# A fused attention and FP4 kernel on eight cores: another order of the quantisation steps, and GpSimd's large operations tied to a step of VectorE

## The chip, the cores and the metric

One Trainium2 chip, eight cores, one launch of the same program on each core. There is no exchange between cores: core i works on batches 2i and 2i+1 of the 16. The time is device microseconds of the slowest core. A comparison of this kernel can tell about 2% from no change.

## The reference

`x` is (16, 2048, 1024) in float32; a core has 4096 rows of it, 32 tiles of 128 rows. Cut to what matters:

```python
xn = layernorm(x)
# s: attention block
qkv = rmsnorm(xn, scale1) @ qkv_w.T
q, k = exp(-0.5*q*q), exp(-0.5*k*k)
out = (q @ (k.T @ v)) / (q @ k.sum() + 1e-6)          # per head, 16 heads of 64
x1  = xn + gamma * (out @ proj_w.T + proj_b)
s   = x1 + gamma * (gelu(rmsnorm(x1, scale2) @ conv1_w.T + conv1_b) @ conv2_w.T + conv2_b)
# g: FP4 feed-forward on the same xn; Q = blockwise FP4 quantise + dequantise, blocks of 16
h = silu(Q(xn) @ Q(w_gate).T) * (Q(xn) @ Q(w_up).T)
g = silu(Q(h) @ Q(w_down).T)
return x + s * g
```

Q takes the largest magnitude of each block of 16, scales by it and rounds to the eight FP4 levels.

## The kernel before

`build()` records every operation with `S.add(engine, fn, waits, ev)` in one global order; each engine then runs its own operations strictly in that order and waits on semaphores for the named events. So an operation that waits holds back everything recorded after it on its engine, and nothing else. The work of a core has three stretches.

**Attention, to about 460 us.** For each tile t: `stats(t)` (two BN_STATS and a BN_AGGR on VectorE, then six small operations on GpSimd that end with `mrs`), `turn(t)` (ScalarE writes the normalised tile `xn1`, SyncE transposes it by DMA), four `kv_group` and, spread over the tiles, `q_group` (eight matmuls each, then ScalarE takes the result out of PSUM), `kv_mm(t)`. SyncE's queue also carries the loads of x (`xa`), the loads of the weights `wst` (`load_w`), the loads `xf` and stores `ob` of the quantisation and the stores of `phi_h`. `cast_w(n)` turns a staged weight into bf16: those of conv1 on ScalarE, those of conv2 and of the projection (16 and 8) on GpSimd as a product with `gm` (L568). `load_w(n)` waits for the cast that held its buffer, on SyncE.

**Attention output and MLP, to about 1030 us.** Eight groups s of four tiles. In the 16 steps oc of `conv1(s, oc)` stand, for the next group's tiles: `prep_xc(t)` (ScalarE normalises x into `xx`, GpSimd adds `gb`, L842), `attn(t)` and `attn_z(t)` (VectorE: den, zz, atz from PSUM), `proj(t)` (x2 on VectorE adds PSUM into `xx`; ScalarE sums the squares; two small operations on GpSimd give rs2) and `proj_xn2(t)` (xn2 on ScalarE, then GpSimd adds `gc2` to `xx`, L945, event x2c). Then `conv2` and `s_out` (VectorE adds PSUM and `xx`).

**FP4 feed-forward, to the end.** Gate, up and down matmuls with `h_task`s in between. Here `late[0]` is true. GpSimd has no work.

**Quantisation.** Each task k is a block of 128 x 1024 (or 768). `stage1`: am (L238), sc (L242), rc (L245), y (L247), all on VectorE; then `coarse` on ScalarE (L256, writes `gam`); `stage2`, VectorE: T (L266, event q_t, reads `gam` and `xf`), nq (L269), out (L272, event q_out, writes `ob`, which SyncE stores). `period(a, b)` interleaves stage1 of task k, letters a, with stage2 of task k-1, letters b, by a string. In the first two stretches `pump(ns)`, called after each group of matmuls, draws as many of these steps as its credit pays for, so the quantisation of the weights and of 17 tiles of x is spread over the matmuls:

```python
            for n, who in enumerate("aabababa" if a.n == 5 else "aababab"):
```

The waits of the ScalarE step are `waits=["q_y%d" % k, opt("q_out%d" % (k - 2))]`.

Of the kernel before, what the change touches and what calls it, by code (L numbers as in the profile page):

```python
# [68 lines left out]
def build():  # L69
    S = Sched()  # L70
# [14 lines left out]
    with ExitStack() as es:  # L85
# [59 lines left out]
        gc2 = gm  # L145
# [63 lines left out]
        late = [False]  # L209
        KX = 28  # L210
# [19 lines left out]
        def stage1(k, W, first, src_ev):  # L230
# [19 lines left out]
            if not late[0]:  # L250
                coarse(k, W)
# [8 lines left out]
        def stage2(k, W, dst, dst_free, post):  # L260
# [13 lines left out]
                  waits=["q_nq%d" % k] + list(dst_free), ev="q_out%d" % k)  # L274
            post(k)
            yield W * 1.06 + 160

        def period(a, b, mid, late_in):
# [3 lines left out]
            for n, who in enumerate("aabababa" if a.n == 5 else "aababab"):  # L282
                src = a if who == "a" else b
                if n == 1:
                    send()
                    mid()
                if n == 5:
                    late_in()
                c = src.step()
                if c:  # L290
                    yield c
# [57 lines left out]
        def both(cur, prev, ahead=None):  # L349
# [26 lines left out]
            for c in period(a, b, mid, late_in):  # L376
                yield c
# [162 lines left out]
        NW4 = 20  # L540

        def wbuf(n):
            return n % 4 if n < NW4 else n % 2

        def load_w(n):
# [3 lines left out]
            before = [m for m in range(n) if wbuf(m) == b]  # L549
            kind, ic, h = wjobs[n]  # L550
# [6 lines left out]
        def cast_w(n):  # L557
# [6 lines left out]
            else:  # L564
# [3 lines left out]
                S.add("gp", lambda p: p.tensor_tensor(dst, wst[b][:], gm[:], op.mult),  # L568
                      waits=["wl%d" % n, "gm", "kvm3"] + w, ev="wc%d" % n)
# [265 lines left out]
        def prep_xc(t):  # L835
# [5 lines left out]
                  waits=["xc%d" % t, "mrs%d" % t], ev="xcn%d" % t)  # L841
            S.add("gp", lambda p: p.tensor_tensor(xb[:], xb[:], gb[:], op.add),  # L842
                  waits=["xcn%d" % t, "gb"], ev="xcg%d" % t)
# [24 lines left out]
        def attn_z(t):  # L868
# [12 lines left out]
            for h0, na, nh, v4 in views:  # L881
# [3 lines left out]
                    waits=["at%d" % t, opt("zz%d" % (t - 2))], ev="den%d" % t)  # L885
            S.add("v", lambda v: v.reciprocal(zz[b][:], den[b][:]),
# [51 lines left out]
        def proj_xn2(t):  # L938
# [6 lines left out]
            S.add("gp", lambda p: p.tensor_tensor(x2b[:], x2b[:], gc2[:], op.add),  # L945
                  waits=["xn2_%d" % t, "gc2"], ev="x2c%d" % t)
# [38 lines left out]
        def s_out(t):  # L985
            n, bks = cur_y[t]
            for hh in range(2):
# [12 lines left out]
        kv_mm(27)  # L1000
        for n, (s, qc) in enumerate([(6, c) for c in range(3, 8)] + [(7, c) for c in range(8)]):
# [77 lines left out]
        for s in range(NS):  # L1079
# [6 lines left out]
            for oc in range(16):  # L1086
# [3 lines left out]
                if nxt and oc in (2, 4, 6, 8):  # L1090
                    prep_xc(4 * (s + 1) + (oc - 2) // 2)
# [282 lines left out]
```

How the kernel before makes its waits and increments, by code:

```python
                def body(eng):  # L1324
                    for fn, waits, inc, amt in S.ops[key]:
                        for smn, val in waits:
                            eng.wait_ge(sems[smn], val)
                        ins = fn(eng)
                        if inc is not None and ins is not None:
                            ins.then_inc(sems[inc], amt)
                    if key == "sy":
                        for smn, val in sorted(S.cnt.items()):
                            eng.wait_ge(sems[smn], val)
```

## Time and profile before

| | |
|---|---|
| runs | 1953.26, 1955.89, 2096.47 us; median 1955.89 |
| profiled execution | 1954.67 us |
| its slowest core | core 4, span 1953.1 us (cores 1941.7 to 1953.1) |
| TensorE | 1852.0 us busy, 95% |
| VectorE | 1631.1 us, 84% |
| ScalarE | 784.9 us, 40% |
| GpSimd | 396.5 us, 20% |

Views are of core 4, and their times count from the start of its span. Idle time of TensorE is read per stretch from its busy time; a matmul group's row counts matmuls, of which a few records are missing. 1.6 us of the profiled time lie outside the span.

### The profile page before, as it was taken

Reading aid. Unit: us, or ns where it says so; the run is one execution under the profiler, and the core shown is the slowest. Engines: PE = TensorE matmul, PEld = TensorE weight load, DVE = VectorE, ACT = ScalarE, POOL = GpSimd, SP = SyncE. Lnnn points to the kernel's source line nnn. Section 1 sums busy time; section 2 is a strip of 40 time slices with the busy share of each in tenths; the row PEclk is TensorE's granted clock in tenths of the full one; section 3 lists DMA queues with packets and bytes.
Section 4 is the critical chain, followed back from the end, with each engine's and each line's share of the span. In section 5 each row is a group of like instructions: output and inputs, shape, how many; then the busy total and the mean of one; then the engine's idle time right before and its main releaser. Section 6 shows DMA issues by size and latency. Waiting matters only on the chain.

```text
span 1953.1 us, 27578 instructions; the slowest of 8 cores (1941.7 to 1953.1 us)
## 1 busy us (share of the span) xinstructions
PE 1852.0 (95%) x8982; PEld 876.4 (45%) x9142; DVE 1631.1 (84%) x1907; ACT 784.9 (40%) x991; POOL 396.5 (20%) x356
## 2 busy tenths in 40 slices
PE   6899999688999999999999999999999999999997
PEld 3344444344444444444444444444444444444443
DVE  5789999868878878778707999999999999999986
ACT  4577686555353353464312222222232222323221
POOL 3246457444252252252200000000000000000000
PEclk9999999899999999999999999999999999999999
DMA  9899898766546547557699333433343333333322
GB/s 304 217 250 251 226 252 244 209 185 170 149 112 194 144 105 184 151 127 197 155 179 189 99 80 104 104 109 76 105 106 90 91 106 89 92 105 101 85 78 68
DMA packets 367261, 287.06 MB, mean 147 GB/s; under 512 B 299024, under 2 KB 308240, under 8 KB 366096
## 3 DMA queue, kind: packets, MB, share of 16 engines
q1 hardware_dynamic: 367120, 285.29, 56.3%
q8 instruction: 75, 1.23, 0.3%
q14 instruction: 66, 0.54, 0.1%
HBM read 153.63 MB, written 59.24 MB: 109 GB/s over the span
## 4 chain that ended last, share of the span: by engine, by line
PE 76%; DVE 6%; issue 6%; DMA 6%; POOL 2%; ACT 2%; SPq 1%; DVEq 0%; ACTq 0%; POOLq 0%
PE PS L1168 31%; PE PS L1213 15%; PE PS L979 11%; PE PS L962 9%; PE PS L914 5%; DMA xa<-x 2%; PE PS L703 1%; PE PS L637 1%; PE PS L671 1%; DVE q_am L238 1%; DVE ob L272 1%; DVE xf L247 1%; DMA wst<-c1T 1%; DMA wqg_h<-ob 1%; PE PS L863 1%
## 5 line engine op out<-in xcount | busy, mean ns | idle before, releaser
L256 ACT ACTIVATE gam<-xf 128x1024 bf16<-128x1024 f32 (+1 forms) x196 | 198.2, 1011 | 502.1 <-DVE xf L247 493.5
L1168 PE MATMUL PS<-wg,xqT 128*128 128x512 bf16 (+1 forms) x1504 | 318.2, 361 | 3.4 <-DVE so L989 1.7
L1168 PE MATMUL PS<-wu,xqT 128*128 128x512 bf16 (+1 forms) x1510 | 317.5, 361 | 1.4
L266 DVE SCALAR_TENSOR_TENSOR xf<-gam,xf 128x1024 f32<-128x1024 bf16 (+1 forms) x196 | 240.5, 1227 | 38.2 <-ACT gam L256 37.9
L272 DVE SCALAR_TENSOR_TENSOR ob<-gam,q_sc 128x1024 bf16<-128x1024 bf16 (+1 forms) x196 | 240.1, 1225 | 4.4 <-DVE gam L269 2.8
L238 DVE TENSOR_REDUCE q_am<-xf 128x64 f32<-128x1024 f32 (+1 forms) x196 | 227.6, 1161 | 18.6 <-DMA xf<-w_gate 4.0
L247 DVE SCALAR_TENSOR_TENSOR xf<-xf,q_rc 128x1024 f32<-128x1024 f32 (+1 forms) x196 | 238.7, 1218 | 1.9
L269 DVE SCALAR_TENSOR_TENSOR gam<-gam,xf 128x1024 bf16<-128x1024 bf16 (+1 forms) x196 | 234.1, 1194 | 2.1
L962 PE MATMUL PS<-xn2T,c1T_s 128*128 128x512 bf16 x1024 | 231.9, 381 | 0.0
L1213 PE MATMUL PS<-wdA,hqT 128*128 128x512 bf16 x998 | 225.4, 380 | 1.8 <-DMA hqT<-ob 0.5
L979 PE MATMUL PS<-c2T_s,hdd 128*128 128x512 bf16 x1000 | 220.9, 379 | 1.3
L1168 PEld LDWEIGHTS PS<-wg,xqT 128*128 128x128 bf16 x1536 | 150.3, 98 | 159.1 <-issue 2.1
L1168 PEld LDWEIGHTS PS<-wu,xqT 128*128 128x128 bf16 x1536 | 150.3, 98 | 153.9
L1178 ACT ACTIVATE sg<-PS 128x1024 f32<-128x1024 f32 (+1 forms) x96 | 90.9, 948 | 182.3 <-PE PS L1168 182.3
L979 PEld LDWEIGHTS PS<-c2T_s,hdd 128*128 128x128 bf16 x1024 | 100.1, 98 | 120.9
L1213 PEld LDWEIGHTS PS<-wdA,hqT 128*128 128x128 bf16 x1024 | 100.5, 98 | 119.4 <-issue 3.1
L962 PEld LDWEIGHTS PS<-xn2T,c1T_s 128*128 128x128 bf16 x1024 | 99.4, 98 | 115.4 <-issue 2.2
L671 PE MATMUL PS<-xn1T,qT_s 128*128 128x512 bf16 x512 | 123.8, 394 | 20.4 <-ACT sq L676 12.6
L842 POOL TENSOR_TENSOR xx<-xx,gb 128x1024 f32<-128x1024 f32 x32 | 83.1, 2606 | 220.4 <-ACT xx L838 220.4
L914 PE MATMUL PS<-projT_s,atzT 128*128 128x512 bf16 x496 | 114.2, 383 | 11.1 <-DVE atz L889 7.3
L1186 DVE TENSOR_TENSOR xf<-PS,sg 128x1024 f32<-128x1024 f32 (+1 forms) x96 | 108.5, 1130 | 14.8 <-PE PS L1168 13.5
L637 PE MATMUL PS<-kT_s,xn1T 128*128 128x512 bf16 x424 | 105.6, 401 | 12.0 <-ACT xn L480 4.2
(91 smaller groups left out, 1840.8 us busy)
## 6 DMA issues: line engine op xcount, KB each, us to landing
xx<-x SPq DMA_DIRECT2D x32, 512.0 KB, 5.1
xf<-x SPq DMA_DIRECT2D x32, 512.0 KB, 4.4
xr<-x SPq DMA_DIRECT2D x32, 512.0 KB, 4.4
out<-xr SPq DMA_DIRECT2D x31, 512.0 KB, 3.2
xa<-x SPq DMA_DIRECT2D x30, 512.0 KB, 6.2
stg<-qkvT SPq DMA_DIRECT2D x24, 512.0 KB, 13.0
xf<-w_gate SPq DMA_DIRECT2D x22, 512.0 KB, 7.9
xf<-w_up SPq DMA_DIRECT2D x22, 512.0 KB, 6.4
```

The source lines that it names most:

```text
L238: S.add("v", lambda v: v.tensor_reduce(am, blk(y), AX, op.max, apply_absolute_value=True), waits=[src_ev, xfree(k)], ev="q_am%d" % k)
L247: S.add("v", lambda v: v.scalar_tensor_tensor(blk(y), blk(y), TIE, bc(rc, nb), op.mult, op.mult), waits=["q_rc%d" % k], ev="q_y%d" % k)
L256: S.add("sc", lambda s: s.activation(gam[k % 2][:, 0:W], xbuf(k)[:, 0:W], AF.Abs, scale=BIG), waits=["q_y%d" % k, opt("q_out%d" % (k - 2)) ...
L266: S.add("v", lambda v: v.scalar_tensor_tensor(y, gm_, FLOOR, y, op.max, op.add), waits=["q_g%d" % k, "q_y%d" % k], ev="q_t%d" % k)
L269: S.add("v", lambda v: v.scalar_tensor_tensor(gm_, gm_, FLOOR, y, op.max, op.subtract), waits=["q_t%d" % k], ev="q_nq%d" % k)
L272: S.add("v", lambda v: v.scalar_tensor_tensor(blk(dst), blk(gm_), -1.0, bc(sc_, nb), op.mult, op.mult), waits=["q_nq%d" % k] + list(dst_fr ...
L671: S.add("pe", lambda pe, ic=ic: pe.matmul(bk, qT[:, ic, P * qc:P * (qc + 1)], xn1T[:, h:h + 4, ic, :], start=(ic == 0), stop=(ic == 7)), w ...
L914: S.add("pe", lambda pe, ic=ic, hh=hh, bk=bk: pe.matmul(bank(bk), atzT[:, t % 4, ic, :], projT[:, ic, 512 * hh:512 * (hh + 1)], start=(ic ...
L962: S.add("pe", lambda pe, ic=ic: pe.matmul(bk, c1T[:, ic, P * oc:P * (oc + 1)], xn2T[:, :, ic, :], start=(ic == 0), stop=(ic == 7)), waits= ...
L979: S.add("pe", lambda pe, ic=ic: pe.matmul(bank(bks[hh]), hdd[:, ic, P * (t % 4):P * (t % 4 + 1)], c2T[:, ic, 512 * hh:512 * (hh + 1)], sta ...
L1168: S.add("pe", lambda pe, wts=wts, bi=bi, j=j, b0=b0, ic=ic: pe.matmul(bank(b0 + j, GB[bi][1]), xqT[t % 3][:, ic, :], wts[bi][:, ic, :], st ...
L1213: S.add("pe", lambda pe, kc=kc, hh=hh, wt=wt, b0=b0: pe.matmul(bank(b0 + hh), hqT[t % 2][:, kc, :], wt, start=(kc == 0), stop=(kc == 21)), ...
```

## The change

Three edits. (1) With four-step tasks the string is "aaababb": VectorE's queue has am, sc, rc of task k, then T of k-1, y of k, nq and out of k-1. `coarse(k)` is no longer recorded behind y but by `absolute()`, at n = 6, just ahead of out. (2) The 24 products of `cast_w` and the 32 additions of `gc2` go to a list `aside`. Each q_out takes one from it, which is recorded on GpSimd behind that step and waits for it. `settle(name)` records without such a wait all up to the one that the next reader needs: 14 of the 24 products get an anchor, 10 don't; all 32 additions do. (3) `prep_xc` stands two steps oc earlier, and its addition of `gb` is recorded in `attn_z` behind den and waits for it, but for tiles 0 to 3 (28 of 32). Instructions are as many as before on each engine, and the queues of TensorE and SyncE have the same order.

```diff
+        aside = []
+        def settle(name):
+            while name not in S.ev:
+                aside.pop(0)(None)
@@ stage1
-            if not late[0]:
-                coarse(k, W)
@@ stage2, behind q_out
+            if aside and not late[0]:
+                aside.pop(0)("q_out%d" % k)
             post(k)
@@ period
-            for n, who in enumerate("aabababa" if a.n == 5 else "aababab"):
+            for n, who in enumerate("aabababa" if a.n == 5 else "aaababb"):
...
+                if n == 6:
+                    absolute()
@@ both
+            def absolute():
+                if cur is not None and not late[0]:
+                    coarse(cur["k"], cur["W"])
@@ load_w
+            if before:
+                settle("wc%d" % before[-1])
@@ cast_w
-                S.add("gp", lambda p: p.tensor_tensor(dst, wst[b][:], gm[:], op.mult),
-                      waits=["wl%d" % n, "gm", "kvm3"] + w, ev="wc%d" % n)
+                if kind == "2" and ic >= 12:
+                    settle("wc%d" % (NW4 - 2))
+                aside.append(lambda at: S.add(
+                    "gp", lambda p: p.tensor_tensor(dst, wst[b][:], gm[:], op.mult),
+                    waits=["wl%d" % n, "gm", "kvm3", at] + w, ev="wc%d" % n))
@@ prep_xc, attn_z
+            if t < 4:
+                add_gb(t, None)
+
+        def add_gb(t, beside):
+            xb = xx[t % 8]
             S.add("gp", lambda p: p.tensor_tensor(xb[:], xb[:], gb[:], op.add),
-                  waits=["xcn%d" % t, "gb"], ev="xcg%d" % t)
+                  waits=["xcn%d" % t, "gb", beside], ev="xcg%d" % t)
...
+            if s:
+                add_gb(t, "den%d" % t)
@@ proj_xn2
-            S.add("gp", lambda p: p.tensor_tensor(x2b[:], x2b[:], gc2[:], op.add),
-                  waits=["xn2_%d" % t, "gc2"], ev="x2c%d" % t)
+            aside.append(lambda at: S.add(
+                "gp", lambda p: p.tensor_tensor(x2b[:], x2b[:], gc2[:], op.add),
+                waits=["xn2_%d" % t, "gc2", at], ev="x2c%d" % t))
@@ s_out
+            settle("x2c%d" % t)
@@ the loop over oc
-                if nxt and oc in (2, 4, 6, 8):
-                    prep_xc(4 * (s + 1) + (oc - 2) // 2)
+                if nxt and oc in (0, 2, 4, 6):
+                    prep_xc(4 * (s + 1) + oc // 2)
```

VectorE in the attention stretch, one period of the quantisation between the statistics of two tiles of x, before (task k works in xf_85, task k-1 in xf_84):

```order
L457 BN_AGGR mv_all<-bst_60 128x2
L272 SCALAR_TENSOR_TENSOR ob_89<-gam_87,q_sc_47 128x1024
L238 TENSOR_REDUCE q_am_45<-xf_85 128x64
L242 TENSOR_SCALAR q_sc_47<-q_am_45 128x64
L266 SCALAR_TENSOR_TENSOR xf_84<-gam_88,xf_84 128x1024
L245 RECIPROCAL q_rc_49<-q_sc_47 128x64
L269 SCALAR_TENSOR_TENSOR gam_88<-gam_88,xf_84 128x1024
L247 SCALAR_TENSOR_TENSOR xf_85<-xf_85,q_rc_49 128x1024
L454 BN_STATS bst_61<-xa_93 128x6
```

and the same place now (line numbers are those of the changed kernel: 278 out, 246 am, 250 sc, 253 rc, 272 T, 255 y, 275 nq):

```order
L474 BN_AGGR mv_all<-bst_60 128x2
L278 SCALAR_TENSOR_TENSOR ob_89<-gam_87,q_sc_47 128x1024
L246 TENSOR_REDUCE q_am_45<-xf_85 128x64
L250 TENSOR_SCALAR q_sc_47<-q_am_45 128x64
L253 RECIPROCAL q_rc_49<-q_sc_47 128x64
L272 SCALAR_TENSOR_TENSOR xf_84<-gam_88,xf_84 128x1024
L255 SCALAR_TENSOR_TENSOR xf_85<-xf_85,q_rc_49 128x1024
L275 SCALAR_TENSOR_TENSOR gam_88<-gam_88,xf_84 128x1024
L471 BN_STATS bst_61<-xa_93 128x6
```

The reciprocal moved ahead of T, and y ahead of nq.

ScalarE early in the attention stretch, round the `coarse` of the second task (gam_88), before (L643 to L652 and L676, L679 take results out of PSUM or follow from that):

```order
L652 CAST vext_99<-PS 128x8x64
L643 ACTIVATE sq<-PS 128x512
L645 ACTIVATE kphi_98<-sq 128x512
L256 ACTIVATE gam_88<-xf_84 128x1024
L643 ACTIVATE sq<-PS 128x512
L645 ACTIVATE kphi_98<-sq 128x512
L676 ACTIVATE sq<-PS 128x512
```

and now:

```order
L674 CAST vext_99<-PS 128x8x64
L665 ACTIVATE sq<-PS 128x512
L667 ACTIVATE kphi_98<-sq 128x512
L665 ACTIVATE sq<-PS 128x512
L667 ACTIVATE kphi_98<-sq 128x512
L262 ACTIVATE gam_88<-xf_84 128x1024
L698 ACTIVATE sq<-PS 128x512
```

`coarse` moved behind the next operation that frees a PSUM bank and its successor. Of the first 37 tasks, those of the attention stretch, 27 move so by one or two operations and 10 stay; of the next 48, 27 move and 21 stay.

GpSimd in the second group of the MLP stretch, before (L931 and L934 are the small operations of `proj`, L945 the addition of `gc2`):

```order
L931 TENSOR_SCALAR ssq_r<-ssq_r 128x1
L934 TENSOR_TENSOR rs_r<-ssq_r,mhalf 128x1
L945 TENSOR_TENSOR xx_150<-xx_150,gm 128x1024
L931 TENSOR_SCALAR ssq_r<-ssq_r 128x1
L934 TENSOR_TENSOR rs_r<-ssq_r,mhalf 128x1
L945 TENSOR_TENSOR xx_151<-xx_151,gm 128x1024
```

and now:

```order
L960 TENSOR_SCALAR ssq_r<-ssq_r 128x1
L963 TENSOR_TENSOR rs_r<-ssq_r,mhalf 128x1
L975 TENSOR_TENSOR xx_149<-xx_149,gm 128x1024
L975 TENSOR_TENSOR xx_150<-xx_150,gm 128x1024
L975 TENSOR_TENSOR xx_151<-xx_151,gm 128x1024
```

The additions of three tiles moved behind the last tile's small operations, into the time of conv2. In the attention stretch the products keep their places between the statistics on GpSimd; only the wait is new there.

## Rows read from the trace of the kernel before

**Rows 1.** Windows: busy us (instructions) of PE, PEld, DVE, ACT, POOL; PEclk, DMA, GB/s.
```profile
48.00:460.00 412.00, 360.85 (x1783) 167.58 (x1811) 350.26 (x417) 278.23 (x407) 202.33 (x198) 0.95 0.85 223
460.00:770.00 310.00, 295.94 (x1453) 138.13 (x1470) 247.01 (x309) 128.26 (x166) 107.97 (x67) 0.99 0.56 153
770.00:1030.00 260.00, 257.33 (x1223) 118.97 (x1242) 164.47 (x205) 108.52 (x134) 69.50 (x46) 0.99 0.69 162
1030.00:1930.00 900.00, 895.32 (x4336) 432.77 (x4423) 836.51 (x930) 247.02 (x253) 0.00 (x0) 1.00 0.39 100
```
**Rows 2.** Chain that ended last, 130 to 275 us: start us, us, what.
```profile
150.68 3.31 POOL c2T_s L568
...
155.81 7.14 DMA xa<-x
```
**Rows 3.** Waits, 48 to 460 us: us in total, times, longest.
```profile
ACT gam L256 <- DVE xf L247: 37.5, 19, 5.5
```
**Rows 4.** Timeline 346 to 349.5 us: start us, us, engine, what [idle before, releaser].
```profile
347.49 1.06 ACT L256 ACTIVATE gam<-xf 128x1024 bf16<-128x1024 f32 x1 [3.67 <-DVE xf L247]
...
349.18 0.59 PE L637 MATMUL PS<-vT_s,xn1T 128*128 128x512 bf16 x2 [1.78 <-ACT sq L643]
```
**Rows 5.** DVE's groups, 48 to 400 us: xcount | busy us, mean ns | idle.
```profile
L266 DVE SCALAR_TENSOR_TENSOR xf<-gam,xf 128x1024 f32<-128x1024 bf16 x37 | 54.0, 1459 | 9.4 <-ACT gam L256 9.4
L272 DVE SCALAR_TENSOR_TENSOR ob<-gam,q_sc 128x1024 bf16<-128x1024 bf16 x37 | 53.9, 1458 | 1.5 <-DMA wqg_h<-ob 1.5
...
L269 DVE SCALAR_TENSOR_TENSOR gam<-gam,xf 128x1024 bf16<-128x1024 bf16 x37 | 47.6, 1285 | 0.0
...
L242 DVE TENSOR_SCALAR q_sc<-q_am 128x64 f32<-128x64 f32 x38 | 13.9, 366 | 3.3
```
**Rows 6.** Timeline 267 to 271 us: a product beside am and sc.
```profile
266.26 1.22 DVE L272 SCALAR_TENSOR_TENSOR ob<-gam,q_sc 128x1024 bf16<-128x1024 bf16 x1
...
267.40 1.21 DVE L238 TENSOR_REDUCE q_am<-xf 128x64 f32<-128x1024 f32 x1
...
267.85 2.36 POOL L568 TENSOR_TENSOR c2T_s<-wst,gm 128x1024 bf16<-128x1024 f32 x1
...
268.71 1.54 DVE L242 TENSOR_SCALAR q_sc<-q_am 128x64 f32<-128x64 f32 x1
```
**Rows 7.** Timeline 196.5 to 201 us: a product at the start of T.
```profile
197.37 0.20 DVE L242 TENSOR_SCALAR q_sc<-q_am 128x64 f32<-128x64 f32 x1
197.48 2.35 POOL L568 TENSOR_TENSOR c2T_s<-wst,gm 128x1024 bf16<-128x1024 f32 x1
197.48 3.43 DVE L266 SCALAR_TENSOR_TENSOR xf<-gam,xf 128x1024 f32<-128x1024 bf16 x1
```
**Rows 8.** Timeline 472 to 479 us: the additions of gb round the last den of a group.
```profile
472.44 3.61 PE L962 MATMUL PS<-xn2T,c1T_s 128*128 128x512 bf16 x16
...
473.17 3.37 DVE L266 SCALAR_TENSOR_TENSOR xf<-gam,xf 128x1024 f32<-128x1024 bf16 x1
...
477.15 1.23 DVE L889 TENSOR_TENSOR atz<-PS,zz 128x1024 bf16<-128x1024 f32 x1 [0.17 <-DVE zz L886]
...
478.74 0.81 PE L914 MATMUL PS<-projT_s,atzT 128*128 128x512 bf16 x3 [2.69 <-DVE atz L889]
```
**Rows 9.** Timeline 614.5 to 618.5 us: an addition of gb that runs beside den and atz.
```profile
615.16 2.85 POOL L842 TENSOR_TENSOR xx<-xx,gb 128x1024 f32<-128x1024 f32 x1 [1.58 <-ACT xx L838]
615.72 0.16 DVE L882 TENSOR_SCALAR den<-PS 128x16 f32<-128x16 f32 x1
...
617.55 1.54 DVE L272 SCALAR_TENSOR_TENSOR ob<-gam,q_sc 128x1024 bf16<-128x1024 bf16 x1
```
**Rows 10.** Timeline 486.5 to 490 us: an addition of gc2 that runs beside x2.
```profile
487.39 2.35 POOL L945 TENSOR_TENSOR xx<-xx,gm 128x1024 f32<-128x1024 f32 x1 [1.44 <-ACT xn L942]
...
489.22 1.29 DVE L921 TENSOR_TENSOR xx<-PS,xx 128x512 f32<-128x512 f32 x2 [3.36 <-PE PS L914]
```
**Rows 11.** DVE's groups, 400 to 1030 us: one of the four.
```profile
L272 DVE SCALAR_TENSOR_TENSOR ob<-gam,q_sc 128x1024 bf16<-128x1024 bf16 x40 | 56.3, 1406 | 0.0
```

More of the change, by code:

```diff
@@ L274, in stage2, with period @@
                   waits=["q_nq%d" % k] + list(dst_free), ev="q_out%d" % k)
+            if aside and not late[0]:
+                aside.pop(0)("q_out%d" % k)
             post(k)
             yield W * 1.06 + 160
-        def period(a, b, mid, late_in):
+        def period(a, b, mid, late_in, absolute):
             a = list_steps(a)
             b = list_steps(b)
-            for n, who in enumerate("aabababa" if a.n == 5 else "aababab"):
+            for n, who in enumerate("aabababa" if a.n == 5 else "aaababb"):
                 src = a if who == "a" else b
@@ L374, in mid @@
                     coarse(prev["k"], prev["W"])
-            for c in period(a, b, mid, late_in):
+            def absolute():
+                if cur is not None and not late[0]:
+                    coarse(cur["k"], cur["W"])
+            for c in period(a, b, mid, late_in, absolute):
                 yield c
@@ L1000, in build @@
         kv_mm(27)
+        settle("wc39")
         for n, (s, qc) in enumerate([(6, c) for c in range(3, 8)] + [(7, c) for c in range(8)]):
```

## The prediction

> **What bounds the kernel now.** I read the windows first, for TensorE's idle time by stretch, then the chain of waits, then the waits by engine, then VectorE's groups and the timeline round single large GpSimd operations.
>
> In the feed-forward stretch TensorE is busy 895.3 of 900 us and GpSimd does nothing; from 770 to 1030 us it is idle 2.7 us [rows 1]. Little can be won from 770 us on. From 48 to 460 us TensorE is idle 412 - 360.9 = 51 us, at a granted clock of 0.95, which is 412 x 0.05 = 21 us more at full speed; from 460 to 770 us it is idle 14 us, and the clock of 0.99 costs 3 us [rows 1]. So about 89 us is all there is, and the question is how much of it the change reaches.
>
> In the attention stretch VectorE is 85% busy and ScalarE 68% [rows 1]: neither is full, but they hand work to each other in queues that can't be passed. Two kinds of stop are visible. ScalarE waits 19 times, 37.5 us, for y before `coarse` [rows 3]; at 347.5 us it had waited 3.67 us there, and the PSUM bank that stood behind it came 1.78 us late for TensorE [rows 4]. And VectorE's operations that read two SBUF tensors stop while a large GpSimd operation runs: T took 3.43 us when a product started with it, 2.2 us more than the 1.22 us of an undisturbed one [rows 6, 7]. A reduction doesn't stop (am took 1.21 us beside a product), but sc behind it does, 1.54 us where 0.20 is usual [rows 6, 7]. After VectorE, GpSimd's product is itself a link of the chain: product 3.31 us, then SyncE's queue, then the load of x, 7.14 us [rows 2].
>
> **The order of the steps.** Nothing is added or removed. y starts one step earlier against the rest of VectorE's queue (nq, about 1.2 us), and `coarse` stands one or two operations later on ScalarE in 27 of 37 cases. Upper bound: each of the 19 waits loses 1.2 us, 23 us of ScalarE's idle time. ScalarE has 412 - 278 = 134 us of idle time here and TensorE 51 us [rows 1], so at most 0.38 us of TensorE's for each of ScalarE's: 9 us. Lower bound: zero, if what ScalarE is then late for is a DMA or GpSimd's `mrs`. I take the middle, **-4 us**, since the one case that I can follow hands on half of its wait (1.78 of 3.67) [rows 4]. From y to its T VectorE now has out, am, sc and rc besides nq, so T's wait for `coarse`, 9.4 us until 400 us [rows 5], should not grow; the pause could cost up to those 9 us again if ScalarE reaches `coarse` later, which is in the range. In the late stretch only the tasks without a first step change their order (15 tiles of x); TensorE has 4.7 us of idle time there [rows 1]. Zero.
>
> **The products in the attention stretch.** Over 1.22 us, T is 37 x 0.24 = 8.9 us too long, out 37 x 0.24 = 8.8, nq 37 x 0.07 = 2.4, and sc over 0.20 us 38 x 0.17 = 6.3 [rows 5]: 26 us for 24 products, 1.1 us each. Ten products have no anchor and stay. Of the 14 others, 13 start (if GpSimd is free) with am, and sc follows. From the case in [rows 6]: the product started 0.45 us after am and held sc until 270.25 us; started with am it would end at 269.8 us and hold sc 0.9 us, with 0.1 us for the release 1.0 us. So 14 x 1.1 = 15 us become 13 us: **-2 us**. Bounds: if the 14 are of the kind of [rows 7] now, 14 x (2.2 - 1.0) = -17 us; if they run free now, +14 us. I stay near the small value because the mean over all 24 is a count and not a choice of cases. Also, GpSimd comes from the six operations of a tile's statistics when it takes the next product, and out stands only one to a few steps behind those statistics on VectorE; in such cases the anchor is over when GpSimd arrives, and the product starts where it did.
>
> What is queued behind a held product on GpSimd is the next tile's statistics, and on SyncE `load_w`, with the transposes and loads of x behind it. I add **+2 us** for two products that come a step late on the chain of [rows 2]; the rival below prices all of them.
>
> **The additions of gb.** Before the last `proj` of a group TensorE waits for atz: at 478.7 us 2.69 us, behind a T of 3.37 us that an addition held up for 2.15 us [rows 8]. Five such gaps, of 2.1 to 2.8 us, one ahead of an `attn` and four ahead of a `proj`, make 12 of the 14 us of 460 to 770 us. Anchored behind den, the addition can't stand in front of its own den. It runs beside zz and atz, which read PSUM; from den's end at 615.88 us and 2.35 us of its own it would end at 618.2 us, and the next VectorE step starts at 617.55 us: 0.65 us held [rows 9, 10]. (The addition there had started 0.1 to 0.2 us earlier and held out 0.33 us.) By the order, am follows atz 5 times of 28, which costs nothing; the other 23 cost 0.65 us, 15 us in all. Three of them lie ahead of the last den of a group, so up to 2 us of lag comes back for the 2.15 us that goes. Each gap then shrinks by 0.2 to 2.1 us; I take 0.8 us: 5 x 0.8 = -4 us, and with 1 of the 3 us of the lower clock **-5 us**.
>
> **The additions of gc2.** Now most run beside x2 and cost VectorE nothing [rows 10]. By the order, 16 of the 32 are anchored ahead of am and sc, 1.0 us each, 16 us; most others have an x2 or s_out step with PSUM in between. Against that, out is 40 x 0.19 = 7.5 us too long now from 400 to 1030 us, one of the four large steps [rows 11], and part of that goes. What hides the rest is VectorE's free time, 310 - 247 = 63 us and 260 - 164 = 96 us [rows 1], and TensorE hardly waits in conv2. Zero; if that cover were gone, up to +16 us. The readers of x2c stand a group later; `settle` stays ahead of them. GpSimd's small operations for rs2 are no longer behind these additions, a gain I can't price above 1 us.
>
> The Trainium skill ("SBUF — State Buffer", Who interferes with whom) says that VectorE and GpSimd share one pair of ports as an exclusive lock that the first comer keeps for the whole instruction, and that a reduction never needs it on this chip. It speaks against this change as a large gain: an operation of 2.35 us placed at a reduction of 1.21 us still holds what comes behind; by it alone the 14 products save only what am covers, and the sum is that of the first rival.
>
> **The sum.** 1954.67 (the profiled run; span 1953.1 and 1.6 outside it) - 4 - 2 + 2 - 5 = 1945.7 us. The median of the runs is 1.2 us above the profiled run: **1947 us**, -0.45%.
>
> **The rivals.**
> *Nothing moves.* The holds are placed elsewhere but last as long (26 us to 24 us, 15 us for the gb additions), ScalarE's shorter waits end in waits for DMAs. For it: VectorE's work is the same and the lock's time too. Against: the atz gaps have a cause that goes. 1951 to 1960 us, say 1956.
> *SyncE comes late.* A held product delays `load_w`, which delays the loads of x and transposes behind it, and VectorE's statistics. Place: the attention stretch, chain of [rows 2]. Price: one VectorE step, 1.2 us, for each of the 14 anchored products, 17 us, over the gain of nothing: 1973 us. It decides if GpSimd is idle when it comes to an anchored product and q_out is then more than a step away; from 14 x 2.8 us it would pass 2%. Against: the ten products whose load is next have no anchor. This is the slower side.
> *The stops were the cause.* All 14 products gain 1.2 us (17 us), the order 9 us, the five gaps their 2.15 us (11 us), 37 us together; some of it falls on the same stretches of the path, so I put it at -30 us: 1926 us (1915 to 1937). For it: 51 us of idle time in pieces that follow these waits. Against: their number, and that a gap's end is mostly another queue.
>
> **How the numbers follow.** Forecast (1937 to 1955) 0.47; nothing moves 0.23; SyncE late 0.12 (1963 to 1982); the large gain 0.16; anything else 0.02. The range that leaves out no more than 2 in 10: 1928 to 1966, which also takes in the pause of T (+9) and part of the uncovered gc2 additions. A measurement of this kernel can tell about 2%, 39 us. Below 1917 us only the far end of the large gain: 0.04. Above 1995 us only SyncE at twice its price: 0.03. Between them 0.93.
>
> **What the profile after would show.** ScalarE's wait for y in 48 to 460 us from 37.5 to about 20 us. No large step beside sc and T at 3.4 us in the anchored cases, but sc at 1.2 us in a dozen or more. The five gaps behind atz below 2 us. The step behind atz 0.3 to 0.7 us too long. TensorE's idle time from 48 to 460 us from 51 to 45 or 48 us. From 1030 us on no difference. The prediction is wrong if the loads of x move onto the chain more often than now, if T waits much more than 9.4 us for `coarse`, or if the atz gaps stay at 2.1 us and more.

## The result, and the profile after

The changed kernel takes 1967.5 us (median of four runs, 1967.12 to 1972.12); the ratio to the kernel before is 1.0067, 95% interval 1.0049 to 1.0085. Forecast were 1947 us and a range up to 1966 us: the change costs 0.7% where it was to gain 0.45%, and lies just above the range. In some executions the cores of a die run at a lower clock; beside the ratio I therefore give, for each kernel, the mean span of those cores of all its executions whose granted clock was 0.983 or more, less the same mean of the kernel before. For the change that is 1961.1 - 1948.0 = +13.1 us; of the kernel before, the cores of one execution are on record beside this result (against the means of 1946.3 to 1947.5 us of the later comparisons it would be 14 or 15 us). The loss is smaller than the 2% that one comparison can tell, but the interval leaves out 1, and the order of the steps costs in every kernel below that has it.

The windows of the kernel after, core 4, the columns of [rows 1]:
```profile
48.00:460.00 412.00, 360.96 (x1789) 167.14 (x1788) 348.31 (x411) 276.57 (x403) 191.82 (x197) 0.93 0.84 222
460.00:770.00 310.00, 295.99 (x1467) 136.64 (x1466) 253.17 (x310) 125.70 (x163) 103.62 (x68) 1.00 0.58 153
770.00:1030.00 260.00, 253.79 (x1223) 116.26 (x1222) 178.86 (x207) 112.91 (x141) 67.61 (x47) 0.99 0.67 155
1030.00:1930.00 900.00, 898.32 (x4413) 431.67 (x4412) 829.88 (x921) 243.20 (x251) 0.00 (x0) 1.00 0.40 101
```
In the feed-forward nothing changes, as forecast. From 48 to 460 us TensorE is idle 51 us as before, where 45 to 48 us were forecast; over the eight cores it was 44 to 51 us before and is 47 to 56 us after. The granted clock is 0.93 there in place of 0.95, but only on this core: the other seven have 0.94 to 0.96 after and 0.95 or 0.96 before. What stands out is VectorE: 6.2 us more in 460 to 770 us and 14.4 us more in 770 to 1030 us than in [rows 1]. The first matmul of the feed-forward begins at 1038.5 us in place of 1026.4; these rows are from the timelines of TensorE, before and after (each in its own fence):
```profile
1026.41 1.89 PE L1168 MATMUL PS<-wg,xqT 128*128 128x512 bf16 x8 [1.68 <-DVE so L989]
```
```profile
1038.49 1.89 PE L1200 MATMUL PS<-wg,xqT 128*128 128x512 bf16 x8 [1.68 <-DVE so L1020]
```
That is 12.1 us later, and core 4's span grew by 10.4 us, so the whole loss lies before the feed-forward.

What was forecast of ScalarE's wait for y came true. Its waits from 48 to 460 us after (us in total, times, longest), with y's to be held against [rows 3]:
```profile
ACT xn L497 <- POOL mrs_all L490: 27.7, 13, 7.0
ACT gam L262 <- DVE xf L255: 20.8, 14, 3.8
```
The wait for y fell from 37.5 to 20.8 us. But `xn` now waits for GpSimd's `mrs`, 27.7 us in 13 cases; before, that row of the same view was
```profile
ACT xn L480 <- POOL mrs_all L473: 11.1, 5, 4.2
```
The two together went from 48.6 to 48.5 us here (48.6 to 54.9 us on the eight cores before, 48.5 to 57.1 us after). One wait took the place of the other. Two other things that the prediction named didn't happen: T's wait for `coarse` fell from 9.4 to 6.3 us, and on the chain from 48 to 460 us the loads of x take less than before (4.4 to 8.6% of it on the eight cores before, at most 4.5% after).

The cause of the loss is seen in one task of VectorE that nothing disturbs. The timeline before (start us, us):
```profile
174.22 1.21 DVE L238 TENSOR_REDUCE q_am<-xf 128x64 f32<-128x1024 f32 x1
175.53 0.20 DVE L242 TENSOR_SCALAR q_sc<-q_am 128x64 f32<-128x64 f32 x1
175.64 1.22 DVE L266 SCALAR_TENSOR_TENSOR xf<-gam,xf 128x1024 f32<-128x1024 bf16 x1
176.78 0.55 DVE L245 RECIPROCAL q_rc<-q_sc 128x64 f32<-128x64 f32 x1
177.24 1.16 DVE L269 SCALAR_TENSOR_TENSOR gam<-gam,xf 128x1024 bf16<-128x1024 bf16 x1
178.32 1.21 DVE L247 SCALAR_TENSOR_TENSOR xf<-xf,q_rc 128x1024 f32<-128x1024 f32 x1
179.45 1.22 DVE L272 SCALAR_TENSOR_TENSOR ob<-gam,q_sc 128x1024 bf16<-128x1024 bf16 x1
```
and after:
```profile
165.39 1.21 DVE L246 TENSOR_REDUCE q_am<-xf 128x64 f32<-128x1024 f32 x1
166.70 0.20 DVE L250 TENSOR_SCALAR q_sc<-q_am 128x64 f32<-128x64 f32 x1
167.00 0.55 DVE L253 RECIPROCAL q_rc<-q_sc 128x64 f32<-128x64 f32 x1
167.47 1.16 DVE L272 SCALAR_TENSOR_TENSOR xf<-gam,xf 128x1024 f32<-128x1024 bf16 x1
168.55 1.21 DVE L255 SCALAR_TENSOR_TENSOR xf<-xf,q_rc 128x1024 f32<-128x1024 f32 x1
169.68 1.22 DVE L275 SCALAR_TENSOR_TENSOR gam<-gam,xf 128x1024 bf16<-128x1024 bf16 x1
171.07 1.23 DVE L278 SCALAR_TENSOR_TENSOR ob<-gam,q_sc 128x1024 bf16<-128x1024 bf16 x1 [0.17 <-DVE gam L275]
```
The durations are the same; read the starts. Neighbours that don't depend on each other overlap: T starts 0.11 us after sc, which takes 0.20, and out 1.13 us after y, less than y's own 1.21. An instruction that reads the output of the one in front of it doesn't overlap it in these traces: rc starts 0.30 us after sc, out 1.39 us after nq, with a stop of 0.17 us that the profile names. Each such reader also waits by semaphore for its producer (`waits=["q_sc%d" % k]`, `waits=["q_nq%d" % k]`), and no run has the one without the other; when this text says that neighbours depend on each other, it means both together. The old string has one such pair (am, sc; 1.31 us), the new one three. From the medians of the starts in both traces (28 to 38 pairs of each kind, 48 to 400 us) a task is 6.37 us before and 6.83 us after, 0.46 us more; the sum of the seven durations says nothing of it.

VectorE's groups from 48 to 400 us, after, against [rows 5]:
```profile
L275 DVE SCALAR_TENSOR_TENSOR gam<-gam,xf 128x1024 bf16<-128x1024 bf16 x37 | 53.7, 1451 | 0.0
L272 DVE SCALAR_TENSOR_TENSOR xf<-gam,xf 128x1024 f32<-128x1024 bf16 x37 | 53.6, 1449 | 6.4 <-ACT gam L262 6.3
...
L278 DVE SCALAR_TENSOR_TENSOR ob<-gam,q_sc 128x1024 bf16<-128x1024 bf16 x36 | 44.5, 1235 | 4.7 <-DVE gam L275 4.1 <-DMA wqg_h<-ob 0.3
```
The holds by GpSimd only moved: out fell from 1458 to 1235 ns, nq rose from 1285 to 1451, sc from 366 to 405, T stayed. From 400 to 1030 us sc stands out; first before, then after:
```profile
L242 DVE TENSOR_SCALAR q_sc<-q_am 128x64 f32<-128x64 f32 x39 | 9.8, 252 | 3.2
```
```profile
L250 DVE TENSOR_SCALAR q_sc<-q_am 128x64 f32<-128x64 f32 x39 | 23.8, 610 | 3.5 <-DVE q_am L246 0.5
```
sc carries 14 us more, with as many instructions.

Who waits for that? VectorE's own waits from 460 to 1030 us, before and after:
```profile
DVE xx L921 <- PE PS L914: 84.5, 27, 4.0
DVE so L989 <- PE PS L979: 49.4, 10, 30.5
```
```profile
DVE xx L950 <- PE PS L943: 72.9, 27, 3.9
DVE so L1020 <- PE PS L1009: 32.1, 4, 26.1
```
`so` is the addition that closes a tile. The sums of its row mislead: besides the one long wait, the last three tiles of the stretch have 5.62 us each, in both kernels (after, two of them lie behind 1030 us). One of the three, before:
```profile
1011.16 1.29 DVE L989 TENSOR_TENSOR so<-PS,xx 128x512 bf16<-128x512 f32 x2 [5.62 <-PE PS L979]
```
In all the groups ahead of the last, VectorE was early for so six times before, 2.0 us in all, and twice after, 0.4 us. There was hardly any lead to lose, and where so comes late, the next `attn` waits for the bank. The timeline after, round 835 us:
```profile
833.83 1.22 DVE L278 SCALAR_TENSOR_TENSOR ob<-gam,q_sc 128x1024 bf16<-128x1024 bf16 x1 [0.17 <-DVE gam L275]
...
836.10 1.28 DVE L1020 TENSOR_TENSOR so<-PS,xx 128x512 bf16<-128x512 f32 x2
...
837.52 0.63 PE L890 MATMUL PS<-kvbd,phq 128*128 128x130 bf16 x8 [2.18 <-DVE q_sc L250]
```
The releaser is named as sc, but so ends at 837.4 us and is what `attn` waits for. Before, TensorE had no stop behind VectorE from 771 us to the first matmul of the feed-forward. Round the additions of gb, after:
```profile
477.88 2.35 POOL L869 TENSOR_TENSOR xx<-xx,gb 128x1024 f32<-128x1024 f32 x1
478.49 1.79 DVE L250 TENSOR_SCALAR q_sc<-q_am 128x64 f32<-128x64 f32 x1
...
482.24 2.34 POOL L869 TENSOR_TENSOR xx<-xx,gb 128x1024 f32<-128x1024 f32 x1 [2.01 <-DVE den L909]
482.62 1.23 DVE L918 TENSOR_TENSOR atz<-PS,zz 128x1024 bf16<-128x1024 f32 x1 [0.17 <-DVE zz L915]
483.77 1.90 DVE L255 SCALAR_TENSOR_TENSOR xf<-xf,q_rc 128x1024 f32<-128x1024 f32 x1
484.00 3.61 PE L943 MATMUL PS<-projT_s,atzT 128*128 128x512 bf16 x16 [2.51 <-DVE atz L918]
```
The step behind atz, y, takes 1.90 us, 0.7 more than alone, as forecast, and no large step is held ahead of atz here any more ([rows 8] had 3.37 us); sc is, for 1.79 us. The stop ahead of `proj` is still 2.51 us. All of them together, in TensorE's waits from 460 to 1030 us after, stand beside the new ones for so:

```profile
PE PS L890 <- DVE atz L918: 7.5, 9, 1.5
PE PS L943 <- DVE atz L918: 5.7, 5, 2.5
PE PS L890 <- DVE so L1020: 4.6, 3, 2.2
```
Ahead of `proj` it was 7.3 us in three cases and 2.8 us in a fourth before, and is 5.7 us now. Ahead of `attn` it was 3.1 us and is 14.3 us (7.5, 4.6 and the 2.2 of 837 us), of which the 6.8 us behind so are the same on all eight cores and had no counterpart before.

### The profile page after: what moved, and what is told of

Read it like the earlier page. It is cut to its first block, busy times and chain, and to the rows that moved or that the text cites. A ratio compares the mean times of both kernels' runs of the same rounds, so it can differ in the third digit from the quotient of the medians.

```text
span 1965.1 us, 27636 instructions; the slowest of 8 cores (1959.1 to 1965.1 us)
## 1 busy us (share of the span) xinstructions
PE 1850.9 (94%) x8982; PEld 874.9 (45%) x9142; DVE 1655.2 (84%) x1907; ACT 783.0 (40%) x991; POOL 378.1 (19%) x356
## 4 chain that ended last, share of the span: by engine, by line
PE 68%; DVE 14%; issue 9%; DMA 3%; ACT 2%; POOL 2%; SPq 1%; DVEq 0%; ACTq 0%; POOLq 0%
PE PS L1200 31%; PE PS L1245 15%; PE PS L992 6%; PE PS L1009 6%; PE PS L943 6%; DVE gam L275 3%; DVE q_am L246 2%; DVE q_sc L250 2%; DVE xf L255 1%; PE PS L725 1%; DVE xf L272 1%; DVE atz L918 1%; PE PS L693 1%; DMA xa<-x 1%; PE PS L659 1%
## 5 line engine op out<-in xcount | busy, mean ns | idle before, releaser
L275 DVE SCALAR_TENSOR_TENSOR gam<-gam,xf 128x1024 bf16<-128x1024 bf16 (+1 forms) x196 | 244.9, 1249 | 2.4 <-DVE q_sc L250 0.4
L278 DVE SCALAR_TENSOR_TENSOR ob<-gam,q_sc 128x1024 bf16<-128x1024 bf16 (+1 forms) x196 | 228.2, 1164 | 15.7 <-DVE gam L275 15.0
L255 DVE SCALAR_TENSOR_TENSOR xf<-xf,q_rc 128x1024 f32<-128x1024 f32 (+1 forms) x196 | 233.8, 1193 | 1.9
L996 ACT ACTIVATE hdd<-PS,c1b_fm 128x512 bf16<-128x512 f32 x128 | 87.0, 679 | 89.1 <-PE PS L992 88.8
L1218 DVE TENSOR_TENSOR xf<-PS,sg 128x1024 f32<-128x1024 f32 (+1 forms) x96 | 108.4, 1129 | 13.6 <-PE PS L1200 12.3
## 6 DMA issues: line engine op xcount, KB each, us to landing
stg<-qkvT SPq DMA_DIRECT2D x24, 512.0 KB, 13.6
```

The costliest lines, as they stand in the source:

```text
L255: S.add("v", lambda v: v.scalar_tensor_tensor(blk(y), blk(y), TIE, bc(rc, nb), op.mult, op.mult), waits=["q_rc%d" % k], ev="q_y%d" % k)
L275: S.add("v", lambda v: v.scalar_tensor_tensor(gm_, gm_, FLOOR, y, op.max, op.subtract), waits=["q_t%d" % k], ev="q_nq%d" % k)
L278: S.add("v", lambda v: v.scalar_tensor_tensor(blk(dst), blk(gm_), -1.0, bc(sc_, nb), op.mult, op.mult), waits=["q_nq%d" % k] + list(dst_fr ...
```

## The experiments

Two theories stood at the start. **A**: the order aaababb makes dependent neighbours, a task is 0.46 us longer. **B**: the GpSimd operations that are tied to steps of VectorE are what costs. C and D came later, in the expectations.

In the table, "cores" is the difference of the mean spans described above (the kernel before: 1946.3 to 1947.5 us in these comparisons; by the spread over cores a mean is good to about 1 us, e13's and e9's a little less). The three stretches are means over such cores of the profiled execution alone: from the first `kv_mm` to the last, from there to the end of the fourth conv2, and to the end of the eighth. The attention stretch differs by some 3 us from core to core, the conv stretches by 1 or 2; the rows of e2, e3, e11 and e14 rest on two cores each, e13's on the two that had 0.982 and 0.983.

| kernel | ratio, 95% | cores, us | attention | groups 0-3 | groups 4-7 |
|---|---|---|---|---|---|
| before | 1 | 0 | 400.4 | 298.5 | 271.0 |
| after | 1.0067 (1.0049-1.0085) | +13.1 | 405.4 | 301.5 | 277.1 |
| e1_order | 1.0123 (1.0099-1.0147) | +20.0 | 406.2 | 301.7 | 280.4 |
| e2_gpsimd | 1.0009 (0.9977-1.0040) | +1.1 | 398.2 | 299.2 | 273.6 |
| e3_coarse_late | 0.9941 (0.9913-0.9968) | -5.9 | 397.2 | 293.7 | 271.2 |
| e4_gb_only | 0.9937 (0.9914-0.9960) | -6.5 | 397.7 | 292.9 | 270.3 |
| e5_all_but_string | 0.9991 (0.9971-1.0011) | -1.8 | 397.1 | 295.7 | 273.6 |
| e6_late_and_gb | 0.9965 (0.9942-0.9987) | -8.4 | 402.4 | 290.6 | 270.3 |
| e7_products | 1.0032 (1.0017-1.0048) | +1.1 | 397.3 | 296.9 | 270.9 |
| e8_gc2 | 1.0055 (1.0038-1.0072) | +9.7 | 397.1 | 306.6 | 274.3 |
| e9_aaabbab | 1.0120 (1.0060-1.0179) | +23.3 | 408.4 | 301.1 | 280.1 |
| e10_string_alone | 1.0034 (1.0008-1.0059) | +16.9 | 407.2 | 298.3 | 279.2 |
| e11_abababa | 1.0009 (0.9982-1.0036) | +4.5 | 406.1 | 292.3 | 276.5 |
| e12_all_but_gc2 | 1.0019 (0.9981-1.0057) | +4.8 | 405.0 | 294.7 | 273.5 |
| e13_longer_task | 1.0234 (1.0176-1.0292) | +48.7 | 413.9 | 303.2 | 275.4 |
| e14_no_gc2_old_order | 0.9936 (0.9897-0.9974) | -8.7 | 399.9 | 290.3 | 270.2 |

**The first four: the change cut at its edits.** `e1_order` is edit 1 alone.
```diff
-            for n, who in enumerate("aabababa" if a.n == 5 else "aababab"):
+            for n, who in enumerate("aabababa" if a.n == 5 else "aaababb"):
+                if n == 6: absolute()        # coarse(k), no longer in stage1
```


> The kernel before with edit 1 alone: the string aaababb and coarse recorded ahead of out; GpSimd as before. Theory A (dependent neighbours: a task of VectorE takes about 0.46 us longer, since rc now follows sc and out follows nq directly): about +9 us of the +13 stand in the attention stretch, so 1.003 to 1.006 of before, and the period of a task is 6.83 us in place of 6.37. Theory B (the anchored GpSimd operations are what costs): no slower than before, 0.996 to 1.000, since ScalarE's waits for y get shorter.


`e2_gpsimd` is edits 2 and 3 alone.

> The kernel before with edits 2 and 3 alone: products, gc2 and gb additions queued to steps of VectorE; the order of the steps as before. Theory A: between 0.997 and 1.002 of before, the gaps behind atz in the MLP stretch shrink, a part is lost to sc steps held by gc2 additions. Theory B: all of the loss is here, 1.005 to 1.009, and the loads of x stand on the chain more often.


`e3_coarse_late` keeps the old string and only records `coarse` at n = 6.

> The kernel before with the place of coarse alone: the old string aababab, but coarse recorded at n = 6, ahead of out. No step of VectorE moves. Theory A: 0.996 to 1.000, ScalarE's wait for y in 48 to 460 us falls from 37.5 to some 25 us. Theory B gives the same here. If it is slower by 0.3% or more, T waiting for coarse is a cause that neither theory has.


`e4_gb_only` is edit 3 alone.

> The kernel before with edit 3 alone: prep_xc two steps oc earlier and the gb additions behind den. Theory A: 0.997 to 0.999, the five gaps behind atz of 2.1 to 2.8 us shrink to 1 to 2 us, and nothing changes to 400 us. Theory B: 1.000 to 1.003, the step behind atz is held in every tile.

The order of steps alone costs more than the whole change, and the three GpSimd parts together cost nothing, so A's account of the loss holds and B, as stated, falls. Only e2 came out in the stretch that A gave for it: e1 lost more than expected, e3 and e4 won more. The string is the difference of e1 and e3, 26 us; `coarse` late is a gain. It is not the gain that I had forecast, though. ScalarE's waits from 48 to 460 us in e3, core 2 (42.4 and 11.1 us on that core before):
```profile
ACT gam L254 <- DVE xf L247: 24.7, 14, 4.3
ACT xn L484 <- POOL mrs_all L477: 19.0, 13, 6.0
```
The attention stretch of e3 is 397.2 us, that of e2, e4, e7 and e8, which leave `coarse` where it was, 397.1 to 398.2: nothing gained there. Its 5 us lie in conv groups 0 to 3 (293.7 against 298.5). The addition of gb gains there too (292.9). TensorE's waits from 460 to 1030 us in e4, where the kernel before had 7.3 and 3.1 us (each has one more stop ahead of `proj` that is put down to rc, 2.5 and 2.8 us):
```profile
PE PS L921 <- DVE atz L896: 3.2, 3, 1.6
PE PS L868 <- DVE atz L896: 2.5, 3, 1.4
```

**The next four: parts put together and split.** `e5_all_but_string` is the change with the old string, `e6_late_and_gb` the two gains together.

> The whole change, except that the seven quantisation steps keep the old order aababab (the coarse step is still given to ScalarE at n = 6, so after y as in the change). Theory A (the loss is made by the order aaababb, which sets instructions behind the one whose output they read, sc before rc and nq before out, 0.46 us more in each of 40 tasks): this kernel is faster than the changed one by about 1% and slightly faster than before, 0.994 to 0.999; VectorE's spacing from sc to the next instruction is 0.11 us and from y to out 1.13 us again, 6.37 us per task. Theory B (the GpSimd operations anchored to VectorE's steps carry the loss together with the new order of ScalarE): it stays at 1.003 or above. The sum of the single parts measured so far (coarse late 0.9941, the GpSimd parts 1.0009) gives 0.995.

> Only the two parts that gained by themselves: the coarse step at n = 6 with the old order of steps (0.9941 alone) and the addition of gb behind den (0.9937 alone). They act in different stretches (ScalarE's wait for y lies in the attention stretch, the hold of atz in the conv groups), so if both theories of their gain hold they add: 0.988, some 1931 to 1936 us on undisturbed cores. If both gains were one and the same (for instance a shift of the whole schedule, or the choice of a chip), it is 0.994 again.


`e7_products` has only the products tied to out, `e8_gc2` only the additions of gc2:
```diff
-            S.add("gp", lambda p: p.tensor_tensor(x2b[:], x2b[:], gc2[:], op.add), ...
+            aside.append(lambda at: S.add("gp", ... waits=["xn2_%d" % t, "gc2", at] ...
```


> Only the products of the weights with gm are anchored to a step out of VectorE; the additions of gc2 and gb and the order of steps are as before. My prediction held a gain of 2 us for it (0.999). If the anchored products are what costs in the GpSimd parts (they hold up the loads of weights and the waits of TensorE in the attention stretch), it is 1.003 or more, with VectorE and TensorE later by 5 us at 455 us of the span. If the cost is the additions of gc2, it is 0.998 to 1.000.

> Only the 32 additions of gc2 are anchored to a step out of VectorE. My prediction priced this at zero, with up to 16 us if its cover is gone: the addition holds VectorE's small step sc 1.1 us longer (so seen behind the change: sc of 0.2 us takes 1.3 us), some 25 times while the conv groups run. If that hold reaches TensorE (the last output step so of a group comes late, and the next attention waits for its bank), it is 1.003 to 1.006 and TensorE shows new idle times of 2 us ahead of the attention of the groups at 540, 835 and 910 us. If VectorE has the time to spare, 0.999 to 1.001.

The old string gives back 15 us of the change (+13.1 to -1.8) at 0.9991, the upper end of what A expected. The products cost 1 us by the cores; the ratio says 3 to 9 us, between the two cases of the expectation and into the one in which the products cost, but the attention stretch, where they run, is not longer than in its neighbours. The additions of gc2 cost 10 us, 8 of them in groups 0 to 3, though nothing else was touched. In e8, core 1, from 460 to 1030 us, sc and then TensorE's waits:
```profile
L247 DVE TENSOR_SCALAR q_sc<-q_am 128x64 f32<-128x64 f32 x35 | 20.7, 591 | 2.9
```
```profile
PE PS L921 <- DVE atz L896: 8.3, 3, 3.3
PE PS L870 <- DVE atz L896: 7.5, 4, 3.2
PE PS L870 <- DVE so L998: 2.6, 3, 1.1
PE PS L870 <- DVE q_sc L247: 1.1, 1, 1.1
```
sc is at 591 ns as in the changed kernel, and the `attn` of a new group waits for so with the old string too, four times (one is put down to sc). VectorE's lead ahead of so isn't smaller in e8 than before (3.3 us in six cases ahead of the last group), and its waits for `proj` are as long (84.5 us); the cost arises at single places in spite of them. The gains of e3 and e4 add only in part: -8.4 where -12.4 was the sum. Both shorten TensorE's waits behind atz, but there they add (from 460 to 1030 us, with those put down to rc: 12.3 to 13.6 us before, 9.6 and 9.8 in e3, 7.3 to 8.2 in e4, 4.8 to 5.9 in e6), so where the rest goes stays open.

**Which property of the order?** `e9_aaabbab` and `e10_string_alone` change the string alone (and leave `coarse` behind y), as does `e11_abababa`. `e12_all_but_gc2` is the change without the tied additions of gc2.

> Only the order of the seven steps is changed, to aaabbab: am, sc, rc, T, nq, y, out, so y comes one step later than in aaababb, where it was in the kernel before, and nq no longer stands in front of out, but T in front of nq. Theory A (an instruction that reads the output of the one before it can't overlap it): sc to rc 0.30 us in place of sc to T 0.11 us, T to nq about 1.39 us in place of rc to nq, so again two dependent neighbours and about 0.4 us more for each task; 1.010 to 1.018, like the order aaababb. Theory C (what costs in aaababb is that y and with it ScalarE's coarse step come two steps earlier, ahead of the normalisations and of the numerators that ScalarE does for TensorE): here y keeps its place, so 0.998 to 1.003.

> Only the order of the seven steps is changed, to aaababb; the coarse step is recorded where it was, directly behind y. Theory A: 1.018, the ratio of the run with both parts of the order (1.0123) over the run with the late coarse step (0.9941); spacing sc to rc 0.30 and nq to out 1.39 us. If the late coarse step and the new order of steps only cost together, it is below 1.008. Theory C (an early coarse step): above 1.018, since here ScalarE gets it even earlier.

> Only the order of the seven steps is changed, to abababa: am, T, sc, nq, rc, out, y. No instruction reads the output of the one in front of it, not even sc that of am, as it does in the kernel before (spacing am to sc 1.32 us where independent neighbours of the same size have 1.13 us). Theory A: 0.19 us less for each of 40 tasks on VectorE, 0.993 to 0.998, unless T, which now comes only one step behind the next am, waits for ScalarE's coarse step of 1.0 us that begins after y: then T's waits for it grow by up to 0.1 us a task and it is 0.998 to 1.003. If the spacing has nothing to do with dependence, am to its successor stays 1.32 us.

> The whole change without the anchoring of the 32 additions of gc2. Alone against the kernel before it cost 0.55%, 10 us on undisturbed cores, 8 of them in the first four conv groups and 3 in the last four. If it costs the same inside the change, this kernel is 1.002, with the conv groups shorter by 10 us than in the changed kernel. If the gap of gc2 is hidden there behind the longer tasks (or the longer tasks behind it), it stays within 0.2% of the changed kernel, 1.005 to 1.009.

e9 leaves y where it was and costs 23 us: C falls. Its T to nq spacing is 1.27 us (I had expected 1.39), its task 6.77 us. e10 costs 16.9 us by the cores, 0.87%, where the ratio says 0.34%. The ratio takes the slowest core of each execution, and the median of that was 1964.6 us for the kernel before in this comparison and 1954.3 us in the one ahead of it; I go by the cores, as the stretches do (14.8 us until the end of group 7), and keep the doubt: by the ratio the string alone would cost 7 us. Either way it is less than the 26 us between e1 and e3, so the string and the late `coarse` cost more together than each by itself. How the string's loss reaches TensorE is seen in groups 4 to 7: from 775 to 1030 us of core 4, where TensorE waited for VectorE in no `attn` or `proj` before, e10 has four stops of 1.9 to 2.4 us behind atz. e10 also shows what became of ScalarE's wait for y with the string alone. Core 4, from 48 to 460 us, against the 37.5 us of [rows 3]:
```profile
ACT gam L256 <- DVE xf L247: 52.1, 25, 4.4
```
The string made that wait longer; it was the later `coarse` that made it shorter (e3).

e11 missed: no neighbours depend on each other, and sc no longer follows am at 1.32 us, but T now waits for `coarse`. VectorE, e11, core 7, from 48 to 460 us:
```profile
DVE xf L266 <- ACT gam L256: 20.8, 30, 4.0
```
Thirty waits in place of five with 9.4 us before; the task came out at 6.55 us, 0.18 us longer than the old one instead of 0.19 us shorter, and the kernel 4.5 us slower. e12 takes 8.3 us off the changed kernel (+13.1 to +4.8): gc2 costs inside the change about what it costs alone.

**Length or place?** All these strings move steps as well. `e13_longer_task` keeps the old one and repeats the reciprocal:
```diff
+            S.add("v", lambda v: v.reciprocal(am, sc_), waits=["q_sc%d" % k], ev="q_rd%d" % k)
             S.add("v", lambda v: v.reciprocal(rc, sc_), waits=["q_sc%d" % k], ev="q_rc%d" % k)
```


> The kernel before, order aababab, with one more reciprocal of the same 64 values in each task, into the buffer q_am that is free by then: a task of VectorE is longer by one such instruction, about 0.45 us, as in the order aaababb, but no step changes its place and no neighbours become dependent. Theory A (length is what costs): 12 to 20 us, 1.006 to 1.010, half of it or more in the attention stretch and the rest in the conv groups. Theory D (the places of the steps cost, not the length): under 4 us, 1.000 to 1.002.


`e14_no_gc2_old_order` is e5 without the tied additions of gc2.

> e5_all_but_string without the anchored additions of gc2: old order of steps, late coarse step, gb behind den, anchored products. If gc2 costs by its hold of the step sc alone, it costs the same 10 us here, and the ratio is 0.994 (e5 had 0.9991), like e6_late_and_gb. If most of its cost was that the additions of gb wait behind it in GpSimd's queue, which the third edit undoes, it is 0.997 to 0.999.

A task of e13, core 4:
```profile
170.80 1.22 DVE L267 SCALAR_TENSOR_TENSOR xf<-gam,xf 128x1024 f32<-128x1024 bf16 x1
171.94 0.55 DVE L245 RECIPROCAL q_am<-q_sc 128x64 f32<-128x64 f32 x1
172.40 0.50 DVE L246 RECIPROCAL q_rc<-q_sc 128x64 f32<-128x64 f32 x1
172.82 1.16 DVE L270 SCALAR_TENSOR_TENSOR gam<-gam,xf 128x1024 bf16<-128x1024 bf16 x1
```
The extra instruction adds 0.41 us (rc to nq falls from 0.46 to 0.41 us). By the end of group 7 e13 has lost 22.6 us (413.9 + 303.2 + 275.4 against 969.9 us), 13.5 of them in the attention stretch: no step changed its place, so length alone makes a loss of the string's size, and D falls. Why 0.41 us of plain length costs more than the string's 0.46 stays open. The total is far above what I expected because the repeated reciprocal also stands in the feed-forward, whose string the change doesn't touch; there another 25 us go, on a VectorE that was 93% busy [rows 1].

Held against the length of a task, from the medians of the starts, the time lost by the end of group 7 in the profiled runs is 14.1 us at 6.83 (after), 14.8 (e10, 6.83), 19.7 (e9, 6.77), 22.6 (e13, 6.78) and 5.0 (e11, 6.55), all less the 969.9 us of the kernel before. It rises with the length but isn't a function of it alone; that e9 loses more than e10 at the shorter task stays open. e14 is 6.9 us ahead of e5, so of gc2's 9.7 us at most 3 came from the old place of the gb additions.

The faster versions are those without the new string and without the tied gc2: e3, e4, e6 and e14, at 0.994 to 0.997, 6 to 9 us ahead of the kernel before and 19 to 22 us ahead of the changed one.

## Why the prediction was wrong

**The order of the steps, -4 us.** This is the step that failed: "Nothing is added or removed." I counted instructions and their durations, and the durations are indeed unchanged. I didn't look at what each instruction's new neighbour writes. The rows for it lay in [rows 6, 7]: T starts 0.11 us after sc, while sc starts 1.3 us after am, whose own duration is 1.21. Two more pairs of that kind, 0.19 us for sc to rc and 0.26 us for nq to out, make 0.46 us a task with a rounding, and VectorE, "85% busy", didn't absorb them. Measured: +20 us alone in place of -4; -5.9 us from `coarse` late, 26 us between e1 and e3, 17 us for the string by itself (7 by the ratio); inside the change the string is 15 us.

The Trainium skill ("VectorE: DVE Perf Modes", The DRAIN you can't avoid) says that the next operation doesn't start until the pipe is empty, that one which isn't held starts earlier, and that in a chain of `tensor_copy` a semaphore after each costs nothing extra. By the last of these the new order would be free, as I had it. The trace disagrees: out starts 0.08 us before the end of y, for which it doesn't wait, and 0.17 us behind the end of nq, for which it does; rc starts 0.10 us behind the end of sc.

The second half of that step failed too. "at most 0.38 us of TensorE's for each of ScalarE's" presumed that a wait removed on ScalarE is gone. The size on ScalarE was forecast rightly (37.5 to 20.8 us), but in part by luck: the bound of 23 us came from y starting a step earlier, and the string alone made that wait longer, 52.1 us; the later `coarse` shortened it. What ScalarE won was given back to `mrs`, the case that I had named as the lower bound (all of it in the change; in e3, 17.7 us less for y came with 7.9 us more for `mrs`). Late `coarse` won 5 us in conv groups 0 to 3, for which the sum had no term.

**The additions of gc2, 0 us.** Measured 7 to 10 us. "What hides the rest is VectorE's free time, 63 and 96 us" took the idle time of a stretch as cover. Of those 159 us, 84.5 are waits for `proj`'s matmuls and 47.4 lie in the last group (one wait of 30.5 us and three of 5.62). Ahead of so in the other groups only 2.0 us were left, and TensorE's new stops behind so and atz stand there. How much of the 84.5 us could have been spent, and where, the runs don't settle: the sum is 72.9 us after, and 84.5 in e8, which lost 10 us all the same. The bound "up to +16 us" did hold, and the 16 additions at 1.0 us fit: sc took 14 us more. I had the size and gave it the wrong cover.

**The products, -2 us, and SyncE late, +2 us.** Measured +1.1 us together by the cores (3 to 9 us by the ratio). The holds moved from out to nq and stayed, as the rival that nothing moves had it. (The 26 us of holds were a little low: nq by itself takes 1.16 us and not 1.22, which adds 2 us.) The Trainium skill ("SBUF — State Buffer", Who interferes with whom) gives the lock to the first comer for its whole instruction; the trace agrees, sc at 1.79 us beside an addition where it takes 0.20 alone.

**The additions of gb, -5 us.** Measured -6.5 us alone, by the mechanism named: large steps no longer hold atz, and the step behind it is 0.7 us longer. TensorE's waits behind atz from 460 to 1030 us fell by some 5 us in e4, where 4 us had been forecast. Of the gaps, one stayed at 2.5 us in the change.

**The sum and the rivals.** The measured single parts, 20.0 for the order and 1.1 for GpSimd, add to 21 us against 13.1. So the GpSimd parts gain 7 us beside the new order and cost 4 us beside the old one with `coarse` late (e3 to e5). That fits a gb addition behind den that protects more when VectorE is late: TensorE's waits behind atz from 460 to 1030 us are 21 to 25 us in e1 and 12 to 15 us after. No run takes that part out of the change alone. The rival on the slower side gave 1963 to 1982 us, and the time falls there, but by luck, through another mechanism: SyncE was not late (e7, and the smaller share of the loads of x on the chain), VectorE was. No rival was about VectorE's own length, so nothing in the range that ended at 1966 stood for it.

## What to carry to other kernels

When instructions of an in-order engine are put in another order, look for pairs in which one reads what the one before it writes, and take the cost from start-to-start spacings of both kinds of pair in the trace, never from durations. Before idle time is used as cover, split it by what it waits for and by where it stands: of 159 us here, 84.5 were waits for matmuls, 47.4 stood in the last group, and 2.0 us was the lead ahead of the step that TensorE waited for afterwards. A wait removed from an engine that isn't the bound should be priced at nothing until it is shown what that engine waits for next.

## What the runs showed of the hardware

On VectorE a 128 x 1024 step starts 1.08 to 1.14 us after an independent one of 1.16 to 1.22 us, 1.27 us after a producer (T to nq, e9) or 1.39 us (nq to out). A small step, sc, lets an independent one start after 0.11 us and its reader after 0.30 us. The cost of such a pair was 0.13 to 0.26 us. In every one of them the reader also waits by semaphore for its producer, also where the profile names no stop; which of the two makes the gap, no run here separates.
